# Context projections regrouped from batch groups into blocks of three full token tiles

## The chip, the cores and the metric

The kernel runs on one core of a Trainium2 chip. The metric is the device time of one launch in microseconds (us); several launches are timed and the median is given. One execution was also recorded by the hardware profiler.

## The reference, cut to what matters

Two transformer layers on x of 16 batches x 256 tokens x 512 features. Only the projections of the first cross-attention are touched. The context has 256 tokens a batch too: the first 77 are "text", the other 179 "image", and each kind has its own weights for keys and values (512 x 1024 each).

```python
ctx_txt = context[:, :TEXT_LEN, :]            # TEXT_LEN = 77
ctx_img = context[:, TEXT_LEN:, :]            # 179 tokens
q    = (x @ Wq).reshape(B, N, HEADS, DIM_HEAD)
k    = (ctx_txt @ Wk).reshape(...);     v    = (ctx_txt @ Wv).reshape(...)
k_ip = (ctx_img @ Wk_ip).reshape(...);  v_ip = (ctx_img @ Wv_ip).reshape(...)
out  = _attend(q, k, v) + _attend(q, k_ip, v_ip)
```

## The kernel before

The program is a row of phases. The first, `project_context` (phase "pr", lines 239 to 568), computes all keys and values of the context and writes them to DRAM: keys transposed to `k_d` (feature rows, 4096 token columns), values to `v_d` (token rows). Meanwhile it normalizes and transposes x (written to `xn_d`) and dequantizes gate weights. `attend_pairs` (phase "at") then reads these arrays. Everything later is untouched.

The tokens of one kind are cut in *blocks*, `context_blocks`: four text blocks of four batches (308 tokens) and then eight image blocks of two batches (358 tokens). A block is a list of runs of context rows, and its tokens are cut in tiles of 128; both sorts have three tiles, the last with 52 or 102 tokens of its own. A matmul of values still runs over 128 tokens there: `skip` counts the ones that it computes a second time, and the store leaves them out.

A block gives *jobs*: eight key jobs ("k", m), each 12 matmuls whose moving side is all tokens of the block, and two value jobs ("v", t, h) for each tile, each 12 matmuls of 512 columns. `product` (lines 194 to 196) makes three matmuls of each, since a value is kept as a high and a low part. So there are 14 jobs a block and 168 in all. TensorE runs the jobs in order; between jobs it transposes ("turns") context tiles of the next block ("c": after jobs 1, 2 and 3 of a block), tiles of x ("x": after jobs 5, 7, 9, 11 of an image block) and gate weights ("w"), four transposes a turn. ScalarE makes the high part of each turn and of each raw weight piece, and takes the even jobs out of PSUM (six banks) to `stage` (six slots); VectorE makes the low parts and takes the odd jobs. VectorE also does the statistics of x (line 443) after job 2 of an image block and the normalization (line 452) after job 3.

SyncE (queue SP) issues every DMA of the phase, in the order of its loop over the jobs: weight pieces two jobs ahead of their split (`load_piece`, a raw piece needs one of three buffers), context rows (`load`, line 366), x (`load_x`, line 371, at job 12 after the start of an image block), and the stores of job j (line 424) once it lies in its slot. Weight pieces 16 to 23 (Wq, Wo) are split at jobs 4, 6, ... 18 counted from the first image block.

Of the kernel before, what the change touches and what calls it, by code (L numbers as in the profile page):

```python
# [23 lines left out]
P = 128  # L24
# [31 lines left out]
class Count:  # L56
# [3 lines left out]
    def __init__(self, eng, sem, base=0):  # L60
        self.eng, self.sem, self.base, self.n = eng, sem, base, 0
# [136 lines left out]

IMG = S - TEXT
EARLY_W = 4  # L200
TB, IB = 4, 2


class Rows:


    def __init__(self, kind, first, n, runs):
        self.kind, self.first, self.n, self.runs = kind, first, n, runs

        self.tiles = [(lo, min(P, n - lo), max(0, lo + P - n)) for lo in range(0, n, P)]  # L210

# [8 lines left out]
        return out  # L220


def context_blocks():
    blocks = []
    for g in range(B // TB):
        blocks.append(Rows("text", g * TB, TB * TEXT, [((g * TB + i) * S, TEXT) for i in range(TB)]))
    for g in range(B // IB):
        blocks.append(Rows("img", g * IB, IB * IMG, [((g * IB + i) * S + TEXT, IMG) for i in range(IB)]))
    return blocks


# [16 lines left out]
def project_context(nc, a, x_in, ctx_in, xn_d, k_d, v_d, wg_d, first, second, ident, neghalf):  # L248


    blocks = context_blocks()
    NBLK, NTX = len(blocks), B // TB
    jobs = [(c, job) for c, block in enumerate(blocks) for job in jobs_of_block(block)]
    first_job = [next(i for i, (c, _) in enumerate(jobs) if c == b) for b in range(NBLK)] + [len(jobs)]
    NJ = len(jobs)
# [30 lines left out]
    with Phase(nc, "pr") as ph:  # L286
# [30 lines left out]
        def stores(j):  # L317

            c, job = jobs[j]
            block = blocks[c]  # L320
            slot = stage[:, j % NST]
            if job[0] == "k":
                each = TEXT if block.kind == "text" else IMG
                off, nb = (0 if block.kind == "text" else TEXT), block.n // each
                cols = slice(block.first * S, (block.first + nb) * S)
                return [(k_d[job[1] * P:(job[1] + 1) * P, cols].rearrange("p (b n) -> p b n", n=S)[:, :, off:off + each],
                         slot[:, 0:block.n].rearrange("p (b n) -> p b n", n=each))]
            lo, count, skip = block.tiles[job[1]]
            cols = slice(job[2] * CT, (job[2] + 1) * CT)
            return [(v_d[row:row + length, cols], slot[skip + at:skip + at + length, :]) for at, row, length in block.pieces(lo, count)]  # L330

        stored_by = [0] * NJ
        per_slot = [0] * NST
# [1 line left out]
            per_slot[j % NST] += 16 * len(stores(j))  # L335
            stored_by[j] = per_slot[j % NST]

        loads = [[(t, piece) for t, (lo, count, skip) in enumerate(block.tiles) for piece in block.pieces(lo - skip, P)] for block in blocks]
        landed_by = [0] * NBLK
        per_half = [0, 0]  # L340
        for c in range(NBLK):
# [17 lines left out]
        with nc.Block() as block_:  # L359
            @block_.sync  # L360
            def _(sp):
                def load(c):
                    if c:
                        sp.wait_ge(t_full, number["c", c - 1, len(blocks[c - 1].tiles) - 1] + 1)
                    for t, (at, row, length) in loads[c]:
                        sp.dma_start(rows[at:at + length, t, :], ctx_in[row:row + length, :]).then_inc(landed[c % 2], 16)

                def load_x(i):
                    if i:
                        sp.wait_ge(t_full, number["x", i - 1, NT - 1] + 1)  # L370
                    sp.dma_start(xrows[:], x_in[i * CT:(i + 1) * CT, :].rearrange("(t p) d -> p t d", p=P)).then_inc(x_ready, 16)

                def load_piece(i):
                    name, k, region = pieces[i]
                    src = a["L0_xattn_" + name]
                    if i >= NRAW:
                        sp.wait_ge(w_lo, i - NRAW + 1)
                    if name == "Wo":
                        sp.dma_start(raw[:, i % NRAW].rearrange("p (a n) -> p a n", n=D),
                                     src[2 * k * P:(2 * k + 2) * P, :].rearrange("(a p) n -> p a n", p=P)).then_inc(raw_ready[i % NRAW], 16)  # L380
                    else:
                        sp.dma_start(raw[:, i % NRAW], src[k * P:(k + 1) * P, :]).then_inc(raw_ready[i % NRAW], 16)

                def load_gate(i):
                    sp.wait_ge(w_lo, len(pieces))
                    if i >= 2:
                        sp.wait_ge(t_full, number["w", i - 2, 0] + 1)
                    sp.dma_start(raw[:, i % 2, 0:D], a["L0_ffn_w_gate"][i * P:(i + 1) * P, :]).then_inc(wr_ready[i % 2], 16)

                def store_aside(n):  # L390
                    after, kind, i, t = turns[n]
                    m = aside[n]
                    sp.wait_ge(t_lo, n + 1)
                    if kind == "w":
                        sp.dma_start(wg_d[i].bitcast(F32), xturned[:, m % NX].rearrange("p a k n -> p (a k n)").bitcast(F32)).then_inc(x_stored[m % NX], 16)
                        return
                    b, half = i * NB + t * P // S, t * P % S
                    sp.dma_start(xn_d[b, :, :, :, half:half + P].rearrange("p a k n -> p (a k) n").bitcast(F32),
                                 xturned[:, m % NX].rearrange("p a k n -> p (a k) n").bitcast(F32)).then_inc(x_stored[m % NX], 16)

                load(0)
                for i in range(RIGHT_AWAY):
                    load_piece(i)
                load(1)
                for j in range(NJ):
                    c = jobs[j][0]
                    for at in range(0 if j == 0 else j + 2, j + 3):
                        for i in piece_at.get(at, []):
                            load_piece(i)
                    if c + 2 < NBLK and j == first_job[c] + len(blocks[c + 1].tiles):  # L410
                        load(c + 2)
                    if j == first_job[NTX - 1]:
                        load_x(0)
                    for i in range(KF):
                        if j == first_job[WFIRST + i // WPER - 1] + WAT[i % WPER] + 1:
                            load_gate(i)
                    if c >= NTX and c + 1 < NBLK and j == first_job[c] + 12:
                        load_x(c - NTX + 1)
                    for n, kind, _, _ in turns_at.get(j - 1, []):
                        if kind != "c":  # L420
                            store_aside(n)
                    sp.wait_ge(job_out[j % 2], j // 2 + 1)
                    for dst, src in stores(j):
                        sp.dma_start(dst, src).then_inc(stored[j % NST], 16)
                for i in range(NST):
                    sp.wait_ge(stored[i], per_slot[i])
                for i in range(NX):
                    sp.wait_ge(x_stored[i], 16 * len(range(i, len(aside), NX)))
# [2483 lines left out]
```

## Time and profile before

| | |
|---|---|
| median of 3 runs | 3357.21 us (3352.15 to 3359.76) |
| the profiled execution | 3357.8 us, span 3356.0 us |
| TensorE busy | 3146.3 us (94%) |
| VectorE, ScalarE, GpSimd busy | 1966.3, 1667.6, 794.6 us |
| projection phase, first product to last | about 22.4 to 445.9 us |
| DMA engines, mean share of the span on SP's queue | 44.9% |

A launch lasts 1.8 us longer than the span of its instructions. Busy time counts a matmul until its modelled end, so matmuls that follow each other overlap in the table; the pace is read from their starts. The rest of the rows stand below, ahead of the prediction.

### The profile page before, as it was taken

How to read it: one execution, taken by the hardware profiler on the slowest of the kernel's cores; microseconds unless marked ns; L12 is line 12 of the kernel's file. 1: busy time of each engine (PE TensorE's matmuls, PEld its weight loads, DVE VectorE, ACT ScalarE, POOL GpSimd, SP SyncE). 2: the span in 40 equal slices, each digit the busy share in tenths (PEclk: the TensorE clock that was granted, in tenths of full speed). 3: DMA queues.
4: the chain of work that ended last, by engine and by line, in shares of the span. 5: the costliest groups of instructions: out<-in, count | busy, mean ns of one | idle time of the engine just before them, and what ended most of it. 6: DMA issues, size and time to landing. Idle time of an engine off the chain costs nothing. (4 is left out here: it accounts for less than half of the span.)

```text
span 3356.0 us, 51210 instructions
## 1 busy us (share of the span) xinstructions
PE 3146.3 (94%) x16793; PEld 2687.9 (80%) x16793; DVE 1966.3 (59%) x3426; ACT 1667.6 (50%) x3210; POOL 794.6 (24%) x881
## 2 busy tenths in 40 slices
PE   7999979999999979999996798996979999999998
PEld 6988969999999968887884576886957888888886
DVE  3255549999999965557888995554843222222221
ACT  3132249999999953336776785564722111111110
POOL 0000038888888830000000200004700000000000
PEclk9999989999999999999998898998989999999999
DMA  6487755555555555556666686444831110001000
GB/s 186 118 249 228 232 172 164 171 179 169 173 166 171 166 181 180 181 171 205 227 217 217 214 262 220 160 159 164 266 110 60 38 38 32 19 26 38 32 26 13
DMA packets 370165, 503.46 MB, mean 150 GB/s; under 512 B 58940, under 2 KB 237420, under 8 KB 366032
## 3 DMA queue, kind: packets, MB, share of 16 engines
q1 hardware_dynamic: 356458, 473.37, 44.9%
q0 software_dynamic: 4768, 18.88, 1.6%
q10 hardware_dynamic: 8720, 8.41, 0.7%
q8 instruction: 124, 2.03, 0.2%
q14 instruction: 95, 0.78, 0.1%
HBM read 292.86 MB, written 174.11 MB: 139 GB/s over the span
## 5 line engine op out<-in xcount | busy, mean ns | idle before, releaser
L2640 DVE SCALAR_TENSOR_TENSOR lf_hT<-lf_hb,lf_hT 128x512 fp32r<-128x512 f32 x128 | 88.5, 692 | 569.5 <-ACT lf_hT L2716 569.5
L2716 ACT ACTIVATE lf_hT<-lf_hb 128x512 fp32r<-128x512 f32 x128 | 76.6, 599 | 667.6 <-PE lf_py L196 638.1
L920 ACT ACTIVATE at_prob<-at_sc,at_nm 128x77 f32<-128x77 f32 (+1 forms) x1024 | 278.7, 387 | 6.9 <-DVE at_nm L804 4.5
L779 POOL TENSOR_TENSOR at_prob<-at_prob,at_rec 128x308 f32<-128x308 f32 (+1 forms) x256 | 261.6, 1044 | 85.2 <-DVE at_rec L817 85.0
L194 PE MATMUL lf_hb<-lf_xT,lf_w 128*128 128x512 f32 x512 | 204.4, 399 | 1.3 <-DVE lf_hT L2640 1.3
L196 PE MATMUL lf_hb<-lf_xT,lf_w 128*128 128x512 f32 x512 | 203.5, 398 | 0.0
L194 PE MATMUL lf_py<-lf_w,lf_hT 128*128 128x512 f32 x512 | 203.1, 397 | 0.0
L196 PE MATMUL lf_py<-lf_w,lf_hT 128*128 128x512 f32 x512 | 203.0, 396 | 0.0
L195 PE MATMUL lf_hb<-lf_xT,lf_w 128*128 128x512 f32 x512 | 202.8, 396 | 0.0
L195 PE MATMUL lf_py<-lf_w,lf_hT 128*128 128x512 f32 x512 | 202.5, 395 | 0.0
L2569 POOL TENSOR_SCALAR lf_var<-lf_mv 128x1 f32<-128x1 f32 x32 | 7.2, 227 | 715.7 <-DVE lf_mv L2592 715.7
L810 DVE TENSOR_REDUCE at_sums<-at_prob 128x4 f32<-128x308 f32 (+1 forms) x256 | 166.0, 676 | 17.7 <-ACT at_prob L920 17.4
L194 PE MATMUL at_qb<-at_xT,xo_Wq 128*128 128x256 f32 x512 | 150.0, 293 | 23.6 <-DVE at_qst L834 12.4
L766 POOL TENSOR_TENSOR at_ks<-at_kr,at_ks 128x512 fp32r<-128x512 f32 x128 | 165.6, 1294 | 13.1 <-ACT at_ks L927 13.1
L194 PE MATMUL dn_py<-qf_wd,dn_om 128*128 128x512 f32 x384 | 150.2, 391 | 16.2 <-DVE dn_om L1984 16.2
L804 DVE TENSOR_REDUCE at_nm<-at_sc 128x4 f32<-128x308 f32 (+1 forms) x256 | 159.6, 665 | 5.8 <-PE at_sc L996 5.8
L821 DVE TENSOR_TENSOR at_pT<-at_tp,at_pT 128x1024 fp32r<-128x1024 f32 x128 | 156.4, 1222 | 3.5 <-ACT at_pT L933 0.4
L194 PE MATMUL pu_bank<-qu_xs,qu_wu 128*128 128x512 f32 x384 | 150.9, 393 | 7.0 <-SPq L1308 5.7
L1019 PE MATMUL at_sc<-at_pT,at_vs 128*128 128x256 f32 x1024 | 153.1, 292 | 1.4 <-issue 1.4
L195 PE MATMUL pu_bank<-qu_xs,qu_wu 128*128 128x512 f32 x384 | 150.3, 391 | 0.0
L196 PE MATMUL pu_bank<-qu_xs,qu_wu 128*128 128x512 f32 x384 | 150.1, 391 | 0.0
L196 PE MATMUL dn_py<-qf_wd,dn_om 128*128 128x512 f32 x384 | 149.9, 390 | 0.0
(346 smaller groups left out, 9232.8 us busy)
## 6 DMA issues: line engine op xcount, KB each, us to landing
at_kr<-k_rows SPq DMA_DIRECT2D x256, 128.0 KB, 2.9
at_qs<-at_qst SPq DMA_DIRECT2D x512, 64.0 KB, 2.0
raw_gate<-pg_stage SPq DMA_DIRECT2D x96, 256.0 KB, 2.0
pu_rg<-raw_gate SPq DMA_DIRECT2D x96, 256.0 KB, 3.3
raw_up<-pu_stage SPq DMA_DIRECT2D x96, 256.0 KB, 2.3
om_raw<-raw_up SPq DMA_DIRECT2D x48, 512.0 KB, 4.5
dn_raw<-raw_up SPq DMA_DIRECT2D x48, 512.0 KB, 3.8
xn_parts<-pr_xturned SPq DMA_DIRECT2D x32, 512.0 KB, 5.0
```

The lines of the kernel that those rows point to most:

```text
L194: pe.matmul(out, lh, rh, start=start, stop=False, **kw)
L195: pe.matmul(out, lh, rl, start=False, stop=False, **kw)
L196: return pe.matmul(out, ll, rh, start=False, stop=stop, **kw)
L766: pool.tensor_tensor(ks[:, n % NK, :, 1, :], kr[:, n % NKR], ks[:, n % NK, :, 0, :].bitcast(F32), ALU.subtract).then_inc(k_low, 1)
L779: ins = pool.tensor_tensor(prob[:, i, :, lo:hi], prob[:, i, :, lo:hi], rec[:, z, g, :].unsqueeze(2).broadcast_to([P, 2 * NTE, hi - lo]), A ...
L804: ins = dve.tensor_reduce(nm[:, n % 2, g, :], sc[n % 2][:, :, lo:hi], AX_X, ALU.max, negate=True)
L810: dve.tensor_reduce(sums[:, z, g, :], prob[:, i, :, SEG[g][0]:SEG[g][1]], AX_X, ALU.add).then_inc(sum_done, 1)
L821: dve.tensor_tensor(pT[:, n % 2, 1], tp[:], pT[:, n % 2, 0].bitcast(F32), ALU.subtract).then_inc(pt_done, 1)
L920: ins = act.activation(prob[:, i, m, lo:hi], sc[n % 2][:, m, lo:hi], ACT.Exp, bias=nm[:, n % 2, g, m:m + 1])
L1019: ins = pe.matmul(attended(s)[:, h, :], vs[:, n % NVP, k, h, :, :].rearrange("p a d -> p (a d)"), pT[:, n % 2, part, k, h * S:(h + 1) * S] ...
L2640: dve.scalar_tensor_tensor(hT[:, i, 1, :], hb[i][:], 0.0, hT[:, i, 0, :].bitcast(F32), ALU.max, ALU.subtract).then_inc(h_done, 1)
L2716: act.activation(hT[:, m % 2, 0, :], hb[m % 2][:], ACT.Relu).then_inc(h_hi, 1)
```

## The change

The tokens of one kind are now one list over all batches, cut at tile borders: text blocks of 256, 384, 384 and 208 tokens, image blocks of 176 and seven times 384. The tiles fall from 12 to 10 for text and from 24 to 23 for images, the jobs from 168 to 162. A block now begins and ends within a batch, so a key job is stored in up to three pieces: the part of a batch at either end, and the full batches together. `spread` cuts a piece of rows in two where its count has no divisor up to 16 that leaves shares of at most 10 rows. In all, key stores go from 96 to 248, value stores from 112 to 158, loads of context rows from 60 to 80. The load of x is now placed by job number alone, so the one at job 12 after the start of the first image block (which has 12 jobs) falls on the first job of the next.

```diff
-TB, IB = 4, 2
+TEXT_BLOCKS = (2 * P, 3 * P, 3 * P, B * TEXT - 8 * P)
+IMG_BLOCKS = (B * IMG - 21 * P,) + 7 * (3 * P,)
...
+def spread(pieces):
+
+    out = []
+    for at, row, count in pieces:
+        share = count // max(d for d in range(1, 17) if count % d == 0)
+        main = count // 16 * 16
+        if share > 10 and main:
+            out += [(at, row, main), (at + main, row + main, count - main)]
+        else:
+            out.append((at, row, count))
+    return out
+
+
 def context_blocks():
+
     blocks = []
-    for g in range(B // TB):
-        blocks.append(Rows("text", g * TB, TB * TEXT, [((g * TB + i) * S, TEXT) for i in range(TB)]))
-    for g in range(B // IB):
-        blocks.append(Rows("img", g * IB, IB * IMG, [((g * IB + i) * S + TEXT, IMG) for i in range(IB)]))
+    for kind, off, length, sizes in (("text", 0, TEXT, TEXT_BLOCKS), ("img", TEXT, IMG, IMG_BLOCKS)):
+        every = Rows(kind, B * length, [(b * S + off, length) for b in range(B)])
+        lo = 0
+        for n in sizes:
+            blocks.append(Rows(kind, n, [(row, count) for _, row, count in every.pieces(lo, n)]))
+            lo += n
+        assert lo == every.n
     return blocks
...
             if job[0] == "k":
                 each = TEXT if block.kind == "text" else IMG
-                off, nb = (0 if block.kind == "text" else TEXT), block.n // each
-                cols = slice(block.first * S, (block.first + nb) * S)
-                return [(k_d[job[1] * P:(job[1] + 1) * P, cols].rearrange("p (b n) -> p b n", n=S)[:, :, off:off + each],
-                         slot[:, 0:block.n].rearrange("p (b n) -> p b n", n=each))]
+                rows_ = slice(job[1] * P, (job[1] + 1) * P)
+                parts = block.pieces(0, block.n)
+                full = [piece for piece in parts if piece[2] == each]
+                out_ = [(k_d[rows_, row:row + count], slot[:, at:at + count]) for at, row, count in parts if count < each]
+                if full:
+                    at, row, nb = full[0][0], full[0][1], len(full)
+                    off = 0 if block.kind == "text" else TEXT
+                    out_.append((k_d[rows_, row - off:row - off + nb * S].rearrange("p (b n) -> p b n", n=S)[:, :, off:off + each],
+                                 slot[:, at:at + nb * each].rearrange("p (b n) -> p b n", n=each)))
+                return out_
...
-            return [(v_d[row:row + length, cols], slot[skip + at:skip + at + length, :]) for at, row, length in block.pieces(lo, count)]
+            return [(v_d[row:row + length, cols], slot[skip + at:skip + at + length, :]) for at, row, length in spread(block.pieces(lo, count))]
...
-        loads = [[(t, piece) for t, (lo, count, skip) in enumerate(block.tiles) for piece in block.pieces(lo - skip, P)] for block in blocks]
+        loads = [[(t, piece) for t, (lo, count, skip) in enumerate(block.tiles) for piece in spread(block.pieces(lo - skip, P))] for block in blocks]
...
-                    if c >= NTX and c + 1 < NBLK and j == first_job[c] + 12:
-                        load_x(c - NTX + 1)
+                    for i in range(NCH - 1):
+                        if j == first_job[NTX + i] + 12:
+                            load_x(i + 1)
```

TensorE at the start of the phase, before (pr_tp holds turns, pr_bank the products of a job, xo_Wq is the buffer in which Wk lies first):

```order
L558 MATMUL pr_tp<-ident,pr_rows 128x128 x12
L194 MATMUL pr_bank<-pr_turned,xo_Wq 128x308
L195 MATMUL pr_bank<-pr_turned,xo_Wq 128x308
L196 MATMUL pr_bank<-pr_turned,xo_Wq 128x308
L194 MATMUL pr_bank<-pr_turned,xo_Wq 128x308
```

and of the change:

```order
L583 MATMUL pr_tp<-ident,pr_rows 128x128 x8
L194 MATMUL pr_bank<-pr_turned,xo_Wq 128x256
L195 MATMUL pr_bank<-pr_turned,xo_Wq 128x256
L196 MATMUL pr_bank<-pr_turned,xo_Wq 128x256
L194 MATMUL pr_bank<-pr_turned,xo_Wq 128x256
```

Two tiles are turned ahead of the first job instead of three, and its products have 256 columns.

SP's queue around the load of the second chunk of x, before (the stores of v_rows are those of the first image block's last value jobs):

```order
L379 DMA pr_raw<-in_L_xattn_Wo_dram 128x2x512
L371 DMA pr_xrows<-in_x_dram 128x4x512
L398 DMA xn_parts<-pr_xturned 1024x1x128
L424 DMA v_rows<-pr_stage 102x512 x2
L379 DMA pr_raw<-in_L_xattn_Wo_dram 128x2x512
L424 DMA k_rows<-pr_stage 128x2x179 x2
```

and of the change:

```order
L403 DMA pr_raw<-in_L_xattn_Wo_dram 128x2x512
L395 DMA pr_xrows<-in_x_dram 128x4x512
L422 DMA xn_parts<-pr_xturned 1024x1x128
L449 DMA k_rows<-pr_stage 128x3
L449 DMA k_rows<-pr_stage 128x23
L449 DMA k_rows<-pr_stage 128x2x179
```

The load of x was followed by the last two value jobs of its block; now it is followed by the key jobs of the next block, each with three stores.

## Rows read from the trace of the kernel before

**Rows 1.** Windows of the phase: stretch, length, each engine's busy time, clock, DMA.

```profile
22.30:32.30 10.00, 6.08 (x27) 5.83 (x28) 0.01 (x1) 0.43 (x1) 0.00 (x0) 0.88 0.85 228
32.30:36.40 4.10, 4.10 (x20) 4.07 (x18) 2.66 (x3) 3.08 (x5) 0.00 (x0) 0.50 0.28 72
156.70:192.50 35.80, 35.80 (x200) 32.35 (x199) 18.63 (x31) 12.72 (x19) 1.28 (x2) 1.00 0.77 231
192.50:445.90 253.40, 252.65 (x1409) 228.24 (x1407) 130.81 (x255) 61.70 (x110) 8.87 (x14) 1.00 0.73 226
```

**Rows 2.** What TensorE waited for, 30 to 445 us: total, times, longest.

```profile
PE pr_tp L558 <- DMA pr_rows<-in_ctx_dram: 3.9, 1, 3.9
PE pr_tp L558 <- DVE pr_xrows L452: 0.8, 1, 0.8
```

**Rows 3.** Timeline of TensorE, 139 to 147 us: start, duration, instruction.

```profile
138.78 0.30 PE L195 MATMUL pr_bank<-pr_turned,xo_Wq 128*128 128x308 f32 x1
...
140.22 0.30 PE L196 MATMUL pr_bank<-pr_turned,xo_Wq 128*128 128x308 f32 x1
140.36 0.40 PE L194 MATMUL pr_bank<-xo_Wo,pr_turned 128*128 128x512 f32 x1
...
145.91 0.40 PE L194 MATMUL pr_bank<-xo_Wo,pr_turned 128*128 128x512 f32 x1
```

**Rows 4.** Timeline of TensorE, 157 to 162 us.

```profile
157.02 0.33 PE L194 MATMUL pr_bank<-pr_turned,pr_w 128*128 128x358 f32 x1
...
160.46 0.33 PE L194 MATMUL pr_bank<-pr_turned,pr_w 128*128 128x358 f32 x1
...
160.96 0.60 PE L558 MATMUL pr_tp<-ident,pr_rows 128*128 128x128 f32 x4
161.31 0.41 PE L194 MATMUL pr_bank<-pr_turned,pr_w 128*128 128x358 f32 x1
```

**Rows 5.** Timeline of TensorE in the next phase, 600 to 606 us.

```profile
603.12 0.28 PE L194 MATMUL at_qb<-at_xT,xo_Wq 128*128 128x256 f32 x1
...
604.51 1.12 PE L996 MATMUL at_sc<-at_ks,at_qs 128*128 128x256 f32 x8
```

**Rows 6.** Timeline of the start, VectorE (DVE).

```profile
19.66 1.28 DVE L473 TENSOR_TENSOR pr_turned<-pr_tp,pr_turned 128x512 fp32r<-128x512 f32 x2
```

**Rows 7.** Timeline of the start, SP's queue.

```profile
13.95 0.33 SPq L382 DMA_DIRECT2D pr_raw<-in_L_xattn_Wk_dram  x1
21.55 2.38 SPq L366 DMA_DIRECT2D pr_rows<-in_ctx_dram  x7
```

**Rows 8.** Timeline of the start, TensorE.

```profile
22.36 0.63 PE L194 MATMUL pr_bank<-pr_turned,xo_Wq 128*128 128x308 f32 x1 [0.84 <-DVE pr_turned L473]
...
31.69 1.12 PE L558 MATMUL pr_tp<-ident,pr_rows 128*128 128x128 f32 x4 [3.86 <-DMA pr_rows<-in_ctx_dram]
...
45.59 0.39 PE L194 MATMUL pr_bank<-xo_Wo,pr_turned 128*128 128x512 f32 x1
```

**Rows 9.** DMA issues on SP, from the tile pr_stage (duration min/median/max).

```profile
L424 SPq DMA_DIRECT2D v_rows<-pr_stage x112: 233/299/2526, 57.3 to 446.7; - x112
L424 SPq DMA_DIRECT2D k_rows<-pr_stage x96: 359/382/2041, 26.3 to 428.1; - x96
```

**Rows 10.** What SP's queue waited for, 230 to 410 us.

```profile
SPq L424 <- DVE pr_stage L482: 55.4, 26, 3.6
SPq L424 <- ACT pr_stage L531: 39.0, 30, 2.0
```

**Rows 11.** The page, DMA queues: packets, MB, share of 16 engines.

```profile
q1 hardware_dynamic: 356458, 473.37, 44.9%
```

**Rows 12.** Splits of Wq pieces on VectorE, from the tile pr_raw.

```profile
L466 DVE SCALAR_TENSOR_TENSOR xo_Wq<-pr_raw,xo_Wq x4: 1225/1226/1226, 169.8 to 185.5; 128x1024 fp32r<-128x1024 f32 x4
```

**Rows 13.** The tile pr_xrows: statistics of x, and its loads from issue to landing.

```profile
L443 DVE BATCH_NORM_STATS2 pr_st<-pr_xrows x32: 674/678/685, 162.8 to 417.1; 128x6 f32<-128x512 f32 x32
...
DMA to landing us min/median/max: 6.4/7.1/8.6
```

More of the change, by code:

```diff
@@ L200, with __init__ @@
 EARLY_W = 4
-TB, IB = 4, 2
+TEXT_BLOCKS = (2 * P, 3 * P, 3 * P, B * TEXT - 8 * P)
+IMG_BLOCKS = (B * IMG - 21 * P,) + 7 * (3 * P,)
 class Rows:
-    def __init__(self, kind, first, n, runs):
-        self.kind, self.first, self.n, self.runs = kind, first, n, runs
+    def __init__(self, kind, n, runs):
+        self.kind, self.n, self.runs = kind, n, runs
         self.tiles = [(lo, min(P, n - lo), max(0, lo + P - n)) for lo in range(0, n, P)]
@@ L251, in project_context @@
     blocks = context_blocks()
-    NBLK, NTX = len(blocks), B // TB
+    NBLK, NTX = len(blocks), len(TEXT_BLOCKS)
     jobs = [(c, job) for c, block in enumerate(blocks) for job in jobs_of_block(block)]
```

## Prediction

> **What bounds the kernel now.** I read the projection phase alone, since nothing behind it changes. First the windows [rows 1]: from 156.7 to 445.9 us TensorE is busy in all but 0.8 us, at full clock, with the DMA engines at 0.73 to 0.77. So TensorE bounds the phase, and what it saves there ends the phase earlier. Then its waits [rows 2]: from 30 us on it waits twice, 3.9 us for context rows and 0.8 us for normalized x. Then the start, where it is not yet the bound [rows 6 to 8].
>
> **The pace of TensorE.** A job's cost is twelve times the distance between starts: 308 columns, ten distances from 138.78 to 140.22, 0.144 us each; 512 columns, 24 distances from 140.36 to 145.91, 0.231 us [rows 3]; 358 columns, 21 distances from 157.02 to 160.46, 0.164 us; a turn of four transposes 161.31 - 160.96 = 0.35 us [rows 4]; 256 columns, twelve distances from 603.12 to 604.51, 0.116 us [rows 5].
>
> **Fewer jobs.** Three tiles less are six value jobs less: 6 x 12 x 0.231 = 16.6 us. Three turns less: 1.1 us. ScalarE, VectorE and SP lose work with them; they are not the bound.
>
> **Key jobs, same columns in other blocks.** Before: 96 x (4 x 0.144 + 8 x 0.164) = 181.2 us. Now I need 384 (between the rows of 358 and 512: 0.175), 256 (0.116), and 208 and 176, which no row shows. If they run on at 2.4 columns a ns, as 256 does with 0.009 us on top, they cost 0.096 and 0.082; the upper end is that they cost what 256 costs. Sum: 96 x (0.116 + 2 x 0.175 + 0.096 + 0.082 + 7 x 0.175) = 179.4 us, a gain of 1.8; with the upper end 184.6, a loss of 3.4. I take the gain, since from 512 down to 256 every row falls with its columns.
>
> **The start.** With two tiles ahead of the first job, the low part of the second is done at 19.66 + 1.28 = 20.94 [rows 6], and no third is waited for: the first product starts there instead of at 22.36, 1.4 us. More follows from SP. The rows of block 1 wait until block 0's last tile is turned, and so were issued at 21.55. Two turns are done before the fourth Wk piece is issued at 13.95 [rows 7], so now they leave some 7 us earlier. That removes the 3.86 us wait at 31.69 [rows 8], and the slow clock that came with it: from 32.3 to 36.4 the granted clock was 0.50, the lower level of 1.2 GHz [rows 1], so half of 4.1 us was lost, 2.0 us. Together 7.3 us. The first value job started at 45.59 [rows 8]; now it wants Wv at about 36 us, and the three Wv pieces behind those rows are also issued some 6 us earlier, so I expect no wait. If Wv comes no earlier, all but the 1.4 us is waited away again; the ends are 0 and 7.3, and I take 7.3, because all these DMAs hang on the same two releases.
>
> **The first two image blocks.** This is where the change takes back. (1) The first has 176 columns: between its job 2, where VectorE begins statistics, and the first turn of x there lay four key jobs and two turns, 4 x 1.97 + 0.7 = 8.6 us; now 4 x 0.98 + 0.7 = 4.6 us. The statistics alone are four of 0.68 us [rows 13], and aggregates, GpSimd's rstd, a split tile and the first normalization follow; I estimate 6 us: 1.5 us of wait. (2) The load of x for the second image block is issued twelve jobs on, now at the first job of that block. Up to the statistics two value jobs, two key jobs and two turns used to follow, 5.5 + 3.9 + 0.7 = 10.1 us, more than the 6.4 to 8.6 us of landing; now two key jobs and two turns, 4.9 us, so x is 2 to 4 us late. Queued behind it on VectorE are a Wo split, the low part of a context tile and the normalization, and TensorE waits for that at the first turn of x. (3) The split pieces come one per (185.5 - 169.8) / 3 = 5.2 us [rows 12]. From job 4 to job 18 TensorE took 35 us, 5.0 for each piece; now 4 x 0.98 + 4 x 2.77 + 6 x 2.10 + 7 turns = 30 us, 4.3 each. Six banks cover most of that lag, but the normalization stands behind it. For (2) and (3) I take 4 us of wait and 2 us of slow clock after it, as at the start. Less the 0.8 us [rows 2] that is already waited: 6.7 us lost. Ends: 0 if the lag is hidden, and 15 if each block waits 6 us and pays the slow clock.
>
> **DMA issues.** Stores of keys grow by 152, of values by 46, loads by 20. At 0.38 and 0.30 us [rows 9] SP issues some 80 us more in the phase. In five image blocks (230 to 410 us) it waited 94.4 us for results to store [rows 10], 18.9 us a block; a block now adds 16 x 0.38 and about 2 us for the rest, 8 us. It stays hidden, and slots come free six jobs (over 12 us) later. The transfers grow by 10,240 short packets. Charged at the mean of SP's queue, 0.449 x 16 x 3356 us / 356458 = 0.068 us [rows 11], they add 43 us to each of the 16 engines at most, 0.1 of the phase: 0.77 becomes 0.87. Nothing on TensorE's path reads these stores before the next phase. So I cost them at nothing; without that cover the price is that of the slower rival.
>
> The Trainium skill (DMA: Bandwidth & Descriptors, Specifications) wants at least 512 B a transfer for line rate and says that below it the engine reads, modifies and writes. By that rule most key stores are the costly sort, and the new pieces of 3 or 23 columns more so; the sum by it would be that of rival E, 3340 to 3380, not 3338. The trace speaks against a great price so far: the text blocks already store keys in runs of 77 columns, 308 B, and TensorE waits for none of them.
>
> **Sum.** -16.6 - 1.1 - 1.8 - 7.3 + 6.7 = -20.1 us on the profiled 3357.8: 3337.7. That run lies 0.6 us above the median of 3357.21, so I say 3338.
>
> **Rivals.** *A: the image blocks hide their lag.* For it: six banks, and 0.8 us of waits before. Against it: x is issued at most 4.9 us ahead. It gives 3357.2 - 26.8 = 3330. *B: the start gains little, or the image blocks pay their upper end.* Wv or Wk_ip pieces come late and TensorE waits for them, or small column counts cost their upper end. For it: the DMA engines are near full at 0.85 between 22.3 and 32.3 us. One such miss costs 5 to 8 us, two 13: 3343 to 3351. *C: no change that can be measured.* Both misses of B with the small columns: 3351 to 3364. *D: slower, SP becomes the bound of the image blocks.* Its longest key store took 2.04 us, its longest value store 2.53 us [rows 9], when the DMA rings were full. A block of 37.5 us has 24 key stores now. With 18.9 us of slack, 1.3 us of longer block and 2 us of other new issues, SP fills the block when a key store takes (18.9 + 1.3 - 2 + 8 x 0.38) / 24 = 0.89 us on average; TensorE then waits for banks behind unstored slots. The kernel gets slower than before when seven blocks lose 20 us more, at 1.01 us; at 1.2 us it is 7 x 24 x 0.31 = 52 us over the sum, 3390. Against it: medians of 0.38 us while the DMA share was already 0.73. *E: as D, but by the DMA engines:* the share has to go from 0.87 to above 1, so a short packet must cost over twice the mean packet of this kernel; beyond that it costs a few us a block, 3340 to 3380.
>
> **How the numbers follow.** Forecast 0.55 (own range 3333 to 3343), A 0.17, B 0.17, C 0.05, D 0.04, E 0.02. The range for 8 in 10 takes in A and the lower half of B: 3327 to 3349. Two tenths of a per cent, about what a measurement can tell here, is 6.7 us: faster below 3350.5. That is forecast, A and nearly all of B, 0.87; same 0.07; slower 0.06.
>
> **What the profile would show.** 162 jobs: the 864 matmuls of value jobs become 792, 0.231 us apart; the 384-column ones about 0.175, those of 176 about 0.08. First product near 21.0, no wait for rows near 30, first value job near 36. One wait for normalized x in the first image block (1 to 2 us) and a longer one in the second. The last product near 445.9 - 20 = 426. Wrong if TensorE shows gaps in the later image blocks released by VectorE or ScalarE out of stored slots (D, E), or if the wait for Wv is long (B).

## The result

The changed kernel took 3330.23 us (median of 4 runs, 3326.48 to 3334.97) against 3355.4 us (4 runs) of the kernel before: ratio 0.9923, 95% interval 0.991 to 0.9935. That is 25 us less; the forecast was 20 less, 3338 with an own range of 3333 to 3343. So the measured time lies inside the range for 8 in 10 (3327 to 3349), but below the forecast's own, at the 3330 of rival A. Run again beside other kernels it gave 0.9921 (0.9908 to 0.9935). The profiled execution is the slowest of the four, 3334.97 us.

The page of the kernel after, its span, TensorE's busy time and SP's queue:

```profile
span 3333.2 us, 51242 instructions
...
PE 3130.7 (94%) x16709; PEld 2675.4 (80%) x16709; DVE 1960.7 (59%) x3420; ACT 1664.1 (50%) x3204; POOL 792.7 (24%) x881
...
q1 hardware_dynamic: 369836, 472.59, 45.3%
```

The span is 22.8 us shorter. SP's queue moves 13,378 packets more (against 356,458, [rows 11]; the forecast counted 10,240) and its share of the DMA engines hardly rises.

The windows of the kernel after, with the columns of [rows 1]; the cuts are the start, the first image block, the second up to 190 us, and the rest:

```profile
18.50:28.50 10.00, 9.90 (x66) 9.90 (x67) 4.72 (x7) 5.15 (x8) 0.00 (x0) 1.00 0.73 232
136.60:161.60 25.00, 24.62 (x171) 22.36 (x170) 15.29 (x28) 9.95 (x16) 1.28 (x2) 1.00 0.74 230
161.60:190.00 28.40, 25.29 (x140) 24.09 (x139) 15.97 (x28) 10.01 (x15) 2.05 (x2) 0.94 0.91 248
190.00:424.90 234.90, 234.90 (x1275) 212.50 (x1273) 118.18 (x229) 54.23 (x97) 7.59 (x12) 1.00 0.74 226
```

The reader sees the same picture as before in the last row: TensorE busy all the time at full clock, DMA share 0.74, so SP's new issues and the short packets cost nothing there, and the DMA engines stay well below the 0.87 that the forecast gave as the most. Of the image stretches 161.6 to 190 us is the one that loses time, with 3.1 us idle and a granted clock of 0.94; before it the wait is 0.4 us. At the start (18.5 to 28.5) there is now next to no gap. The clock of 1.00 in that row must not be taken at its word, as the starts of products show (first two lines after, last two before):

```profile
18.98 0.41 PE L195 MATMUL pr_bank<-pr_turned,xo_Wq 128*128 128x256 f32 x1
...
23.25 0.38 PE L194 MATMUL pr_bank<-pr_turned,xo_Wq 128*128 128x256 f32 x1
```

```profile
22.78 0.46 PE L195 MATMUL pr_bank<-pr_turned,xo_Wq 128*128 128x308 f32 x1
...
26.12 0.43 PE L196 MATMUL pr_bank<-pr_turned,xo_Wq 128*128 128x308 f32 x1
```

They are (23.25 - 18.98) / 20 = 0.214 us apart, later 0.117; before, (26.12 - 22.78) / 13 = 0.257 and later 0.142. By that both kernels run their first four to five us at about half pace, that of the lower level of the clock, after TensorE had done next to nothing for 9 us; the clock column doesn't show it. The change takes nothing from this part.

What TensorE waited for from 30 to 445 us, to hold against [rows 2]:

```profile
PE pr_tp L583 <- DVE pr_xrows L477: 3.5, 2, 3.1
...
PE pr_tp L583 <- DVE pr_turned L498: 1.2, 1, 1.2
```

The wait for context rows is gone; the one for normalized x has grown from 0.8 to 3.5 us, 3.1 of them at one place.

TensorE's timeline, the lines on which the pace and the start of the phase rest:

```profile
7.69 1.97 PE L583 MATMUL pr_tp<-ident,pr_rows 128*128 128x128 f32 x8 [7.69 <-DMA pr_rows<-in_ctx_dram]
18.60 0.58 PE L194 MATMUL pr_bank<-pr_turned,xo_Wq 128*128 128x256 f32 x1 [8.95 <-DVE pr_turned L498]
...
28.19 0.28 PE L194 MATMUL pr_bank<-pr_turned,xo_Wq 128*128 128x256 f32 x1
...
33.10 0.28 PE L194 MATMUL pr_bank<-pr_turned,xo_Wq 128*128 128x256 f32 x1
...
33.45 0.40 PE L194 MATMUL pr_bank<-xo_Wo,pr_turned 128*128 128x512 f32 x1
...
60.27 0.34 PE L194 MATMUL pr_bank<-pr_turned,xo_Wq 128*128 128x384 f32 x1
...
63.39 0.34 PE L194 MATMUL pr_bank<-pr_turned,xo_Wq 128*128 128x384 f32 x1
...
143.71 0.28 PE L194 MATMUL pr_bank<-pr_turned,pr_w 128*128 128x176 f32 x1
...
145.72 0.27 PE L194 MATMUL pr_bank<-pr_turned,pr_w 128*128 128x176 f32 x1
...
335.48 0.39 PE L194 MATMUL pr_bank<-pr_w,pr_turned 128*128 128x512 f32 x1
...
338.88 0.39 PE L194 MATMUL pr_bank<-pr_w,pr_turned 128*128 128x512 f32 x1
```

By the distances, as in [rows 3 to 5]: 256 columns (33.10 - 28.19) / 42 = 0.117 us, 384 columns (63.39 - 60.27) / 18 = 0.173, 176 columns (145.72 - 143.71) / 18 = 0.112, 512 columns (338.88 - 335.48) / 15 = 0.227. These are single stretches. The means over all neighbouring starts of a shape (without those over 1.15 times the median) are 0.117, 0.174, 0.111 and 0.2286, and 0.112 for 208 columns; before, 0.142 for 308, 0.164 for 358 and 0.2313 for 512. The first product starts at 18.60, the first value job at 33.45; before 22.36 and 45.59 [rows 8].

SP's queue in the kernel after: the rows of block 1, and the step from the last store of the phase to the first load of the next:

```profile
11.45 3.81 SPq L390 DMA_DIRECT2D pr_rows<-in_ctx_dram  x9
...
425.87 0.32 SPq L449 DMA_DIRECT2D v_rows<-pr_stage  x1
428.53 0.32 SPq L698 DMA_DIRECT2D at_xT<-xn_parts  x1
```

The rows leave at 11.45 us instead of 21.55 [rows 7]. Added up along TensorE: the first value job comes 12.1 us earlier, the last product starts at 424.72 instead of 445.56, 20.8 us earlier, and the first product of the next phase at 434.09 instead of 457.15, 23.1 us earlier. Behind that nothing of size changes (22.8 us at the end).

How far two executions of one kernel differ inside the phase is seen from after_again, which is the changed kernel once more. Starts in us, each from one profiled execution; the last three kernels are experiments of the next section:

| kernel | first product | first value job | first image product | last product |
|---|---|---|---|---|
| before | 22.36 | 45.59 | 157.02 | 445.56 |
| after | 18.60 | 33.45 | 136.80 | 424.72 |
| after_again | 19.23 | 34.08 | 138.04 | 423.31 |
| a_rowslate | 17.91 | 35.90 | 142.18 | 426.76 |
| a_smalllast | 19.24 | 33.62 | 136.83 | 426.61 |
| a_earlyx | 18.67 | 34.11 | 139.12 | 423.04 |

The last product of the same kernel moved by 1.4 us, so a difference of that size between two rows says nothing.

### The profile page after: what moved, and what is told of

Its sections match the earlier page's. It is cut to its first block and busy times, and to the rows that moved or that the text cites. A ratio compares the mean times of both kernels' runs of the same rounds, so it can differ in the third digit from the quotient of the medians.

```text
span 3333.2 us, 51242 instructions
## 1 busy us (share of the span) xinstructions
PE 3130.7 (94%) x16709; PEld 2675.4 (80%) x16709; DVE 1960.7 (59%) x3420; ACT 1664.1 (50%) x3204; POOL 792.7 (24%) x881
## 5 line engine op out<-in xcount | busy, mean ns | idle before, releaser
L194 PE MATMUL dn_py<-qf_wd,dn_om 128*128 128x512 f32 x384 | 150.5, 392 | 16.0 <-DVE dn_om L2009 16.0
L194 PE MATMUL pu_bank<-qu_xs,qu_wu 128*128 128x512 f32 x384 | 150.7, 393 | 6.8 <-SPq L1333 5.6
L195 PE MATMUL dn_py<-qf_wd,dn_om 128*128 128x512 f32 x384 | 150.3, 392 | 0.0
L196 PE MATMUL dn_py<-qf_wd,dn_om 128*128 128x512 f32 x384 | 150.3, 391 | 0.0
L195 PE MATMUL pu_bank<-qu_xs,qu_wu 128*128 128x512 f32 x384 | 150.2, 391 | 0.0
```

The lines of the kernel that those rows point to most:

```text
L194: pe.matmul(out, lh, rh, start=start, stop=False, **kw)
L195: pe.matmul(out, lh, rl, start=False, stop=False, **kw)
L196: return pe.matmul(out, ll, rh, start=False, stop=stop, **kw)
```

## The experiments

Each was timed beside the kernel before on the same chip; ratios are to that kernel, with 95% intervals.

**Does the row length of the buffer of turned tokens matter?** The value matmuls sped up from 0.231 to 0.227 us although they are the same instructions; what differs is that their stationary operand lies in rows of 384 columns, not 358. Two kernels change that number alone.

```diff
 # b_wide384, from the kernel before
-    WIDE = max(b.n for b in blocks)
+    WIDE = 384
 # a_wide390, from the kernel after
-    WIDE = max(b.n for b in blocks)
+    WIDE = 390
```

> The kernel before, with one number changed: the rows of the buffer of turned tokens are 384 columns long instead of 358, with the same blocks and jobs. In the profile of the change the value matmuls of 512 columns start 0.227 us apart, not 0.231 as before. Theory of the layout: the row length (358 columns are 1432 bytes, no multiple of 64; 384 are 1536) slows the read of the operands from this buffer; then the spacing of the 864 value matmuls falls to about 0.227, that of 358 columns by 0.001 to 0.003, and the time by 3 to 8 us (ratio 0.998 to 0.999). Rival, the spacing fell for another reason, as where the skipped last tile starts (column 230 of 358) or the other traffic: nothing moves here, ratio 1.000, spacing 0.231.

> The changed kernel with rows of turned tokens of 390 columns instead of 384 (1560 bytes, no multiple of 64). Theory of the layout: the spacing of the 792 value matmuls goes from 0.227 back towards 0.231 (3 us), the key matmuls lose a little too, ratio to the kernel before 0.993 to 0.995 instead of 0.992. Rival: nothing moves, 0.227 stays.

Measured: b_wide384 0.9993 (0.9984 to 1.0002), a_wide390 0.9927 (0.9913 to 0.9942). The times can't tell them from their parents, but the tile pr_bank can. Its row for the second of each three value matmuls (min/median/max ns), first in the kernel before, then b_wide384, a_wide390 and the kernel after:

```profile
L195 PE MATMUL pr_bank<-pr_w,pr_turned x192: 388/393/402, 175.2 to 445.3; 128*128 128x512 f32 x192
```

```profile
L195 PE MATMUL pr_bank<-pr_w,pr_turned x192: 387/389/398, 172.9 to 444.4; 128*128 128x512 f32 x192
```

```profile
L195 PE MATMUL pr_bank<-pr_w,pr_turned x184: 389/393/403, 150.7 to 423.8; 128*128 128x512 f32 x184
```

```profile
L195 PE MATMUL pr_bank<-pr_w,pr_turned x184: 387/389/398, 150.4 to 424.5; 128*128 128x512 f32 x184
```

The median is 393 ns with rows of 358 or 390 columns and 389 with 384, in either kernel. The mean distance of all value matmuls goes the same way: 0.2313 us before, 0.2291 in b_wide384; 0.2286 after, 0.2318 in a_wide390. So the row length sets it, in both directions, and the rival (that it came with something else of the change) falls. It is a small part of the gain: 792 x (0.2313 - 0.2286) = 2.1 us. Why the row length matters wasn't tried.

**Does the early issue of the rows carry the gain at the start?**

```diff
 # a_rowslate, from the kernel after
                 for i in range(RIGHT_AWAY):
                     load_piece(i)
+                sp.wait_ge(w_lo, RIGHT_AWAY)
                 load(1)
```

> The changed kernel, but SP issues the context rows of the second block only once all four Wk pieces are split, which is about when they were issued before the change (near 20 us instead of 11.5). Theory of the prediction: the early issue of these rows, and of Wv behind them, is what removed the wait of 3.9 us and the slow clock; then TensorE waits for rows again (3 to 5 us near 28 us), the first value job starts 5 to 9 us later than at 33.5, and the time is 5 to 8 us above the changed kernel's. Rival: the start is bound by when the weights can be read from DRAM in any case, and the first value job moves by less than 2 us.

Measured: 3333.91 us, 0.9929 (0.9916 to 0.9941). The rows were issued at 16.68 us (Wk itself was split sooner than before, so the delay was 5.2 us and not the 9 I wanted), TensorE waited 1.9 us for them, its clock was low again for a part of the stretch (0.85 from 17.9 to 27 us), and the first value job moved from 33.45 to 35.90, 1.8 to 2.5 us later than in the two profiles of the changed kernel. The wait and the low clock come back as the theory says, but half or less of the 5 to 9 us expected. In full time the run can't be told from the changed kernel (5 to 8 us expected). The issue time is one cause of the gain at the start; this run doesn't show it to be all.

**Is the loss in the image blocks due to the short block standing first?**

```diff
 # a_smalllast, from the kernel after
-IMG_BLOCKS = (B * IMG - 21 * P,) + 7 * (3 * P,)
+IMG_BLOCKS = 7 * (3 * P,) + (B * IMG - 21 * P,)
...
-    turns += [(first_job[NTX + i] + 5 + 2 * t, "x", i, t) for i in range(NCH) for t in range(NT)]
-    WFIRST, WPER, WAT = NTX + 2, KF // (NCH - 2), (6, 12)
+    turns += [(first_job[NTX + i] + 5 + 2 * t - (i == NCH - 1 and t == 3), "x", i, t) for i in range(NCH) for t in range(NT)]
+    WFIRST, WPER, WAT = NTX + 2, KF // (NCH - 2), (6, 10)
```

> The changed kernel with the image block of 176 tokens last instead of first (the turns of x and of gate weights in a block of 12 jobs are placed one or two jobs earlier so that they fit). Theory: the waits of 0.4 and 3.1 us for normalized x and the slow clock of 2 us after them come from the short first image block, which leaves the load of the next x two key jobs ahead of its use; with it last they vanish and the last product comes 4 to 7 us earlier, ratio 0.990 to 0.991. Rival: splits of Wq and Wo pieces on VectorE hold the normalization anyway, the wait stays above 2 us and the time at 0.992.

Measured: 3334.98 us, 0.994 (0.9925 to 0.9954). A miss. (The profiled execution took 3329.43 us, the fastest of six.) The waits in the first image blocks are gone, but the timelines of TensorE and VectorE show their like in the short block itself, now the last:

```profile
405.45 1.11 PE L583 MATMUL pr_tp<-ident,pr_xrows 128*128 128x128 f32 x4 [2.44 <-DVE pr_xrows L477]
```

```profile
400.27 2.48 DVE L468 BATCH_NORM_STATS2 pr_st<-pr_xrows 128x6 f32<-128x512 f32 x4 [2.24 <-DMA pr_xrows<-in_x_dram]
```

After it the granted clock was 0.77 from 400 to 410 us and 0.65 from 410 to 418. That low clock costs 0.23 x 10 + 0.35 x 8 = 5.1 us, more than the 3.5 us of waits that the move took away. The last product came at 426.61, 1.9 to 3.3 us later than in the changed kernel. Standing first, the short block has its x early: the load is issued at 116.6 us and the statistics start at 141.3. Standing last, it gets x from a load that comes 2.2 us late for VectorE, and TensorE's wait is 2.4 us instead of 0.4. So this run moves a late load of x to another place, and doesn't tell how much of the loss is due to the short block by itself.

So the load of x behind the short block was moved alone. In the kernel after, VectorE's timeline shows that load as the releaser:

```profile
173.18 2.47 DVE L468 BATCH_NORM_STATS2 pr_st<-pr_xrows 128x6 f32<-128x512 f32 x4 [5.01 <-DMA pr_xrows<-in_x_dram]
```

```diff
 # a_earlyx, from the kernel after
-    turns += [(first_job[NTX + i] + 5 + 2 * t, "x", i, t) for i in range(NCH) for t in range(NT)]
+    turns += [(first_job[NTX + i] + ((5, 7, 8, 9)[t] if i == 0 else 5 + 2 * t), "x", i, t) for i in range(NCH) for t in range(NT)]
...
-                        if j == first_job[NTX + i] + 12:
+                        if j == first_job[NTX + i] + (12 if i else 10):
```

> The changed kernel with the turns of x in the first image block after jobs 5, 7, 8 and 9 (not 5, 7, 9, 11), so that the load of the next x is issued at job 10 and not 12, two value jobs (5.5 us) earlier. Theory: VectorE's wait of 5.0 us for that load, TensorE's wait of 3.1 us behind it and the low clock after it vanish, the last product comes 4 to 6 us earlier than 424.7, ratio 0.990 to 0.991. Rival: the splits of Wo pieces or the full DMA engines (share 0.96 at that place) hold the same turn, and less than 2 us comes back.

Measured: 3329.94 us, 0.9916 (0.9899 to 0.9933). VectorE's wait for x fell from 5.0 to 0.4 us and TensorE's from 3.5 to 1.0, as the theory says. The last product came at 423.04 us, against 424.72 and 423.31 in the two profiles of the changed kernel. Counted from the first image product, which leaves out what the text blocks did, the image blocks took 283.9 us against 287.9 and 285.3. So the late load is worth 1.4 to 4.0 us, where 4 to 6 were expected. The two profiles differ mostly by the clock: in the first, 3.1 us of wait were followed by a low clock that cost 28.4 x 0.06 = 1.7 us, in the second 2.0 us of wait were followed by none. The place is shown, its price isn't known better than that. The interval overlaps the changed kernel's, so I don't call it faster.

**What does the division of pieces do?** First taken from the change, then put alone on the kernel before.

```diff
 # a_nospread, from the kernel after (b_spread: the function and its two calls on the kernel before)
-        if share > 10 and main:
+        if False:
```

> The changed kernel with the pieces of rows left whole (blocks and jobs as changed). Theory: the first context rows landed at 7.7 us instead of 10.6, and the last store of values before the next phase was over in 1.6 us instead of 4.5, because pieces like 51 or 102 rows ran in few shares and now run in many; then without the division the first rows land later again (51 rows stay whole: 9 to 11 us) and the first product comes 2 to 3 us later, ratio 0.993 instead of 0.992. Rival: the earlier landing comes from there being one piece less in the first load and from the run; the first product stays at 18 to 19 us.

> The kernel before with the division of pieces alone. Theory: first rows at 8 instead of 10.6 us, so the first product 1 to 3 us earlier than 22.4, and the wait of SP for the last store (102 rows, now 96 and 6) falls from 4.5 to under 2.5 us, so the next phase starts 10 us after the last product and not 11.6; ratio 0.998 to 0.999. Rival: nothing moves beyond 1 us, ratio 1.000, and SP pays 0.3 us more for each of the added issues.

Measured: a_nospread 3396.15 us, 1.0112 (1.0096 to 1.0128); b_spread 3349.09 us, 0.9978 (0.9969 to 0.9988). The first was a miss by over 60 us (ratio 0.993 expected): the new blocks without the division are slower than the kernel before. What was expected of the start hardly came either: the first rows landed at 8.81 us (9 to 11 expected), the first product came at 19.44, at most 0.8 us later and not 2 to 3. The waits name the cause (total, times, longest):

```profile
ACT pr_stage L556 <- DMA k_rows<-pr_stage: 46.2, 7, 11.4
DVE pr_stage L507 <- DMA k_rows<-pr_stage: 36.1, 5, 10.6
...
ACT pr_stage L556 <- DMA v_rows<-pr_stage: 32.4, 7, 12.4
...
DVE pr_stage L507 <- DMA v_rows<-pr_stage: 29.2, 5, 10.6
```

These sum to 143.9 us; in the kernel before the only wait of this kind was one of 0.8, in the kernel after there is none. ScalarE and VectorE wait for a slot of `stage` whose store has not landed, six jobs after it was issued, and TensorE stops behind them. Its own waits from 30 to 492 us, and a window:

```profile
PE pr_tp L583 <- DVE pr_xturned L498: 23.8, 5, 8.6
PE pr_tp L583 <- DVE pr_xrows L477: 13.9, 3, 9.4
PE pr_tp L583 <- DVE pr_raw L1137: 8.7, 5, 2.9
PE pr_tp L583 <- DVE pr_turned L498: 7.8, 2, 5.6
```

```profile
144.00:491.50 347.50, 298.93 (x1584) 268.25 (x1583) 149.00 (x284) 73.06 (x129) 10.92 (x16) 0.94 0.64 191
```

That is 54.2 us against 4.7 in the kernel after, and a clock of 0.94. The DMA engines have room (0.64). The tile pr_stage gives the issues of SP:

```profile
L449 SPq DMA_DIRECT2D k_rows<-pr_stage x248: 319/447/10152, 22.8 to 474.6; - x124
L449 SPq DMA_DIRECT2D v_rows<-pr_stage x126: 214/350/8627, 48.9 to 492.7; - x126
```

A single issue took up to 10.2 us, with a median of 0.4. Cutting at tile borders makes pieces of 127, 103, 101, 79 and 53 rows, counts whose only equal shares are single rows or one whole. The trace shows one at work. The second of these two stores has 127 rows (254 KB) and is issued at 402.7 us in 0.3 us; the key store right behind it, the first of the eighteen, is the one that takes 10.2 us:

```profile
402.11 0.90 SPq L449 DMA_DIRECT2D v_rows<-pr_stage  x2
403.05 20.91 SPq L449 DMA_DIRECT2D k_rows<-pr_stage  x18
```

The DMA engines from 405 to 409 us, as a window and by queue (packets, MB, share of 16 engines):

```profile
405.00:409.00 4.00, 4.00 (x26) 3.97 (x25) 3.46 (x11) 0.60 (x1) 1.27 (x2) 1.00 0.07 26
q1 hardware_dynamic: 50, 0.10, 6.6%
```

50 packets of 2 KB in 4 us, 26 GB/s, a share of one in sixteen: one engine moves rows one after the other and the other fifteen have nothing. At 26 GB/s 254 KB take 9.8 us, about as long as SP stood. So what a piece without shares costs is not its own issue but the work behind it in the queue. The Trainium skill (DMA: Bandwidth & Descriptors, Why a DMA increments its semaphore by 16 and not by 1) says that a DMA from SP runs on the largest number of engines up to 16 that divides the slowest dimension of both its sides, one for 127 partitions. The trace agrees: 6.6% of sixteen engines here.

On the kernel before the division gains 7 us: the profile of b_spread has the first rows landed at 9.39 us instead of about 10.6, and a wait for the rows of block 1 of 0.17 us instead of 3.86 [rows 8]:

```profile
9.39 1.97 PE L571 MATMUL pr_tp<-ident,pr_rows 128*128 128x128 f32 x8 [9.39 <-DMA pr_rows<-in_ctx_dram]
...
28.02 0.66 PE L571 MATMUL pr_tp<-ident,pr_rows 128*128 128x128 f32 x4 [0.17 <-DMA pr_rows<-in_ctx_dram]
```

The first value job started at 41.87, 3.7 us earlier (in b_wide384, whose start is that of the kernel before, it came at 43.71, so up to 1.9 of them can be the execution), and the first product of the next phase came 9.8 us after the last one of this instead of 11.6 (SP's wait for the last stores: 1.5 us, before 4.5). So of the gain of b_spread up to half is at the start and a quarter at the end; the rest lies between.

**Which pieces, and loads or stores?**

```diff
 # a_share20, from the kernel after
-        if share > 10 and main:
+        if share > 20 and main:
 # a_stores_div: loads of context rows whole
-for piece in spread(block.pieces(lo - skip, P))]
+for piece in block.pieces(lo - skip, P)]
 # a_loads_div: value stores whole
-for at, row, length in spread(block.pieces(lo, count))]
+for at, row, length in block.pieces(lo, count)]
```

> The changed kernel, dividing only pieces whose largest equal share is over 20 rows (counts like 127, 103, 101, 79, 74, 53, 125, 23) and leaving those of 17 or 19 (51, 102, 76) whole, as the kernel before had them. Theory: the 66 us that undivided pieces cost come from the few that run in one or two shares (127 rows of 2 KB one after the other, SP issues of up to 10 us); then nearly all is back, ratio 0.992 to 0.994, and the first rows, with 51 whole, still land late. Rival: the many pieces of 17 to 19 rows count as well, and half or more of the loss stays, ratio above 1.000.

> The changed kernel with value stores divided and loads of context rows whole. Theory: stores free the slots of stage that VectorE and ScalarE waited for (143.8 us of waits on DMAs of k_rows and v_rows without any division), and there are two of each store for one load, so most of the loss goes: ratio 0.993 to 1.001. Rival: a long load holds the in-order queue as much as a long store, and the split of the loss is even, near 1.003.

> The changed kernel with loads of context rows divided and value stores whole. Theory: most of the loss of the undivided kernel stays, ratio 1.003 to 1.011. Rival, the loads are the ones that count: ratio under 1.000.

> The changed kernel as it is, measured beside the three others: 0.991 to 0.9935 as at first. If it lies outside, differences of 0.001 between these runs tell nothing.

| kernel | median us | ratio, interval | last product |
|---|---|---|---|
| after_again | 3329.68 | 0.9921, 0.9908 to 0.9935 | 423.31 |
| a_share20 | 3329.85 | 0.9919, 0.9906 to 0.9933 | 423.58 |
| a_stores_div | 3345.79 | 0.9965, 0.9952 to 0.9979 | 438.68 |
| a_loads_div | 3359.43 | 1.0007, 0.9998 to 1.0016 | 455.5 |
| a_nospread | 3396.15 | 1.0112, 1.0096 to 1.0128 | 491.57 |

Pieces of 17 and 19 rows a share may stay whole: the whole loss comes from those with over 20 rows in a share, eleven pieces, each stored in two halves of the columns and loaded once. Whole stores cost 30 us (a_loads_div against after_again; its ratio is below the 1.003 to 1.011 expected), whole loads 16, both 66. They are more together than one by one; both go through SP's one queue in order, but that this is the reason is not shown.

**How far is SP from being the bound?** Key stores in two halves of 64 partitions, the same bytes with twice the issues.

```diff
 # a_keystores2, from the kernel after
-                return out_
+                return [(d[h:h + 64], s_[h:h + 64]) for d, s_ in out_ for h in (0, 64)]
```

> The changed kernel with every key store cut in two halves of 64 partitions: 496 instead of 248 issues, same bytes. Theory of the prediction (SP has room; it fills an image block when 24 key stores take 0.89 us each): 48 stores of 0.3 to 0.45 us, 14 to 22 us a block, just about fill the room, so the time moves by 0 to 10 us, ratio 0.992 to 0.995. Rival, the issues of SP are already near the bound in the changed kernel: TensorE waits in each image block, 5 us or more a block, ratio above 1.000.

Measured: 3445.88 us, 1.0268 (1.0252 to 1.0283), 116 us above the changed kernel. The tile pr_stage and what SP's queue waited for from 200 to 530 us, of this kernel:

```profile
L449 SPq DMA_DIRECT2D k_rows<-pr_stage x496: 445/597/2547, 21.8 to 522.0; - x166
```

```profile
SPq L449 <- ACT pr_stage L556: 5.2, 6, 2.2
SPq L449 <- DVE pr_stage L507: 3.5, 7, 1.0
```

and the window:

```profile
200.00:530.00 330.00, 272.82 (x1365) 243.48 (x1363) 130.86 (x253) 60.89 (x108) 9.63 (x14) 0.92 0.61 176
```

To hold against the same views of the kernel after, the waits from 190 to 425 us:

```profile
L449 SPq DMA_DIRECT2D k_rows<-pr_stage x248: 319/433/2968, 22.0 to 407.8; - x124
```

```profile
SPq L449 <- DVE pr_stage L507: 38.7, 29, 2.5
SPq L449 <- ACT pr_stage L556: 31.9, 28, 1.6
```

In the kernel after SP still waits 70.6 of 235 us for results; before, it waited 132.5 of 253 (192 to 446 us). With doubled stores it waits 8.7 of 330, while the DMA engines are at 0.61 (0.74 in the kernel after): SP's issuing is the bound, and not the engines. Half a store doesn't issue in half the time, it took 0.60 us instead of 0.43, so an image block has 48 x 0.60 = 29 us of key stores. The forecast put the edge at 24 x 0.89 = 21 us, and this run lies beyond it on the slow side. My expectation of 0 to 10 us was wrong because it took the issues at 0.3 to 0.45 us. Why an issue of fewer bytes takes longer wasn't tried.

## Why the prediction was right, point by point

- **Fewer jobs**, -16.6 us: right. The value jobs lost six, and besides became quicker by 0.0027 us a matmul, 2.1 us, through the length of the buffer's rows; no term of the sum had that. Of the three turns (-1.1) one stands ahead of the first product and is in the term of the start already, so only 0.7 us count here.
- **Key jobs**, -1.8 us: mis-sized, with the wrong sign. With the mean distances 308 columns cost 0.142 (0.144 taken), 384 cost 0.174 (0.175), but 208 and 176 cost 0.112 and 0.111, not 0.096 and 0.082. The sum is 180.6 us before and 96 x (0.117 + 2 x 0.174 + 0.112 + 0.111 + 7 x 0.174) = 183.0 after, a loss of 2.4. The upper end (the cost of 256) was the better guess: below 256 columns the distance hardly falls.
- **The start**, -7.3 us: right in place, too small. The first value job came 12.1 us earlier; 2.4 of that is its shorter key jobs (96 x (0.142 - 0.117)), so 9.7 us went: the wait of 3.9, the low clock of 2.0 after it, and 3.8 by which the first product came earlier. Only this last was off (1.4 forecast). The prediction took the last low part of the two tiles where it stood, ending at 20.94; in the kernel after it is

```profile
17.27 1.28 DVE L498 TENSOR_TENSOR pr_turned<-pr_tp,pr_turned 128x512 fp32r<-128x512 f32 x2
```

  and ends at 18.55. It stands behind the split of the fourth Wk piece, which began on ScalarE at 15.04 instead of 17.43 us, and the Wk pieces stand behind the first rows in SP's queue, which had landed at 7.69 instead of 10.64. With 51 rows whole the rows land at 8.50 us (a_share20), with the division but three tiles at 9.39 (b_spread), so both the division and the smaller first block bring the rows earlier. For the first product the division counts little: it came at 19.18 in a_share20 and at 19.23 in after_again. That the smaller load is what brings Wk earlier is argued, not shown.
- **The image blocks**, +6.7 us: right in mechanism. x came 5.0 us late for VectorE (forecast 2 to 4), TensorE waited 0.4 us in the first block (1.5) and 3.1 in the second (4). The last product came 20.8 us earlier, so the terms above leave for the losses 16.6 + 2.1 + 0.7 + 9.7 - 2.4 - 20.8 = 5.9 us. The trace accounts for it: waits of 0.4 and 3.1, one of 1.2 in a text block that nobody forecast, and 1.7 of low clock, less the 0.8 of before, are 5.6. The late load of x is worth 1.4 to 4.0 of them by a_earlyx.
- **The end of the phase** was no term. The next phase starts 2.2 us sooner behind the last product, since SP waits 1.6 us for the last stores and not 4.5. That isn't the division: a_nospread has the same 1.6. The last tile now has 128 rows of its own and not 102, so the last stores are pieces that the division leaves alone. b_spread, which divides the 102, gains 1.8 us at the same place. (In b_wide384, with the stores of the kernel before, the step was 0.8 us shorter too, so the change is worth 1.4 to 2.2 us here.)
- **DMA issues at nothing**: right for this kernel and wrong as an argument. I named SP's slack and the six slots as the cover, and priced the loss of it by a store's duration, but left out that only the division keeps pieces of 127 or 53 rows from running whole. Without it the change is 1.1% slower, rival D by another road: not the number of issues but a few pieces on one engine each.

Against the sum of -20.1 us the profiled runs lie 22.8 us apart: 2.4 more from the start, 2.2 from the end, 2.1 from the pace of the value matmuls, 0.8 less lost to waits and clock, but 4.2 less from the key jobs and 0.4 less from the turns. The medians lie 25 us apart, within the interval. So the closeness is in part luck: two terms that were missing and one that was too small made good one with the wrong sign. And though the time is rival A's 3330, A did not happen: it had the image blocks hide their lag, and they lost 5.9 us.

## What to carry to other kernels

Where a cut makes pieces of odd row counts, divide each so that it has many equal shares (up to 19 rows in each cost nothing here) before it goes into an in-order queue: the few pieces with over 20 rows a share turned a gain of 25 us into a loss of 40. Fewer and fuller tiles pay by the job, but a short block pays back a part, because what was timed by job number (loads, statistics) then has less time ahead of it. Before reading a difference of 1 or 2 us inside a phase, look at a second profile of the same kernel. Count the issuing queue's waits before adding issues: SP waited half its time, in the changed kernel still 30% of it, and doubling the key stores overran it.

## What the hardware showed that I had not expected

- Mean distances between matmuls at full clock: 512 columns 0.229 to 0.231 us, 384 0.174, 256 0.117, 208 0.112, 176 0.111. Below 256 columns a matmul got hardly cheaper.
- A stationary operand from rows of 384 columns (1536 bytes) took 389 ns in the median, from rows of 358 or 390 columns (1432, 1560 bytes) 393 ns, with the same instructions.
- A store of 127 rows of 2 KB kept one of sixteen DMA engines busy (share 6.6%, 26 GB/s) and the key store behind it took SP 10.2 us to issue; the medians are 0.35 to 0.45 us.
- Halving the partitions of a store, 128 to 64, raised the median issue on SP from 0.43 to 0.60 us. SP became the bound with the DMA engines at 0.61.
- The first products of the phase were 0.214 us apart for 4.5 us and then 0.117, while the profile's clock column reads 1.00 for both.
- Undivided stores cost 30 us, undivided loads 16, both together 66.
